# Dense stage of a graph-network kernel: one root computation for three groups, a chain spread over nine rounds, sums in six banks; counting and second edge layer rearranged

## The reference, cut to what matters

```python
h = jnp.maximum(_layernorm(x, axis=-1), 0.0)
x = x + _L0_gnn_ref(h, edge_index, edge_attr_32, ...)   # messages, gates, update, LayerNorm with gain and shift
h = jnp.maximum(_layernorm(x, axis=-1), 0.0)
x = x + _L1_gnn_ref(h, ..., edge_attr_96, src, dst)     # relu(e @ Wm1 + bm1) @ Wm2 + bm2, times the drop mask, summed by dst
h = jnp.maximum(_layernorm(x, axis=-1), 0.0)
x = x + _L2_gnn_ref(h, edge_index, L2_gnn_W, L2_gnn_b)  # mean over in-edges
h = jnp.maximum(_layernorm(x, axis=-1), 0.0)
x = x + _L3_gnn_ref(h, src, dst, ...)                   # three convolutions with degree norms
```

## Time and profile before

| | us |
|---|---|
| median of 3 runs (lowest, highest) | 6119.12 (6116.01, 6123.38) |
| the profiled execution, its own time | 6117.6 |
| its span, first to last instruction | 6115.7 |
| PE, DVE, ACT, POOL busy in the span | 4559.9, 4229.4, 3505.4, 3410.0 |

### The profile page before, as it was taken

The page is one execution under the profiler, slowest core; times in us unless marked ns, Lnnn a source line. Parts: engine busy times, 40 slices in busy tenths (PEclk is TensorE's granted clock), DMA queues, the critical chain, the costliest instruction groups (busy, mean ns, idle before and its releaser), DMA issues. The chain is left out here.

```text
span 6115.7 us, 115642 instructions
## 1 busy us (share of the span) xinstructions
PE 4559.9 (75%) x22351; PEld 2931.6 (48%) x22351; DVE 4229.4 (69%) x13899; ACT 3505.4 (57%) x8824; POOL 3410.0 (56%) x3543
## 2 busy tenths in 40 slices
PE   5776888888799999799999788878888984222222
PEld 1223555555444444466666566656656663222221
DVE  5667888888788888777777688878876663222222
ACT  6996666666699999555555455545545552111110
POOL 0004666666654443344343566566657776777777
PEclk9999999999999999899999787778778885555555
DMA  0002333333344443455555577656657773222222
GB/s 18 0 0 67 101 105 102 104 103 105 98 96 94 94 94 86 105 143 142 141 142 137 150 188 193 181 148 163 163 144 183 184 187 89 61 64 66 63 67 57
DMA packets 1144861, 677.32 MB, mean 111 GB/s; under 512 B 898421, under 2 KB 1096833, under 8 KB 1144744
## 3 DMA queue, kind: packets, MB, share of 16 engines
q1 hardware_dynamic: 1031784, 527.07, 31.7%
q0 software_dynamic: 112960, 148.99, 11.7%
HBM read 445.59 MB, written 232.61 MB: 111 GB/s over the span
## 5 line engine op out<-in xcount | busy, mean ns | idle before, releaser
L724 POOL DMA_INDIRECT xs<-t,idx x1176 | 1110.5, 944 | 951.5 <-DMA idx<-at 573.4
L1197 PE MATMUL bank<-ident,msg 128*96 128x128 f32 (+1 forms) x1568 | 305.5, 329 | 856.5 <-ACT msg L992 771.8
L724 POOL DMA_INDIRECT xs<-c,idx x784 | 763.9, 974 | 291.6 <-issue 233.2
L992 ACT ACTIVATE msg<-xs,now 128x96 f32<-128x96 f32 x784 | 229.3, 364 | 1071.4 <-DMA xs<-c,idx 715.3
L1041 PE MATMUL bank<-cols,before 128*128 128x384 f32 x1756 | 734.0, 520 | 17.3 <-DVE wu_out L1334 14.1
L1495 DVE TENSOR_TENSOR_SCAN aggT<-goes,aggT,bank 96x512 f32<-96x512 f16 (+1 forms) x490 | 620.7, 1267 | 133.9 <-PE bank L1150 115.0
L1197 PEld LDWEIGHTS bank<-ident,msg 128*96 128x96 f32 (+1 forms) x1568 | 218.6, 163 | 1022.7 <-ACT msg L992 650.1
L1208 PE MATMUL bank<-w,aggT 96*128 96x96 f32 (+1 forms) x3136 | 549.9, 334 | 105.2 <-DVE aggT L1495 104.6
L1670 DVE SCALAR_TENSOR_TENSOR y<-bank,now,rows 128x96 f32<-128x96 f32 x392 | 97.2, 310 | 719.1 <-PE bank L1208 719.1
L724 POOL DMA_INDIRECT xd<-in_x_dram,idx x392 | 373.9, 954 | 395.5 <-DVE xn L1565 228.6
L1208 PEld LDWEIGHTS bank<-w,aggT 96*128 96x128 f32 (+1 forms) x3136 | 517.3, 249 | 130.9 <-issue 88.6
(11 more groups left out here) (233 smaller groups left out, 10943.2 us busy)
## 6 DMA issues: line engine op xcount, KB each, us to landing
t<-xn SPq DMA_DIRECT2D x294, 192.0 KB, 2.2
xd<-t SPq DMA_DIRECT2D x294, 192.0 KB, 3.5
goes<-goes_d SPq DMA_DIRECT2D x392, 128.0 KB
xd<-in_x_dram SPq DMA_DIRECT2D x196, 192.0 KB
t<-xo SPq DMA_DIRECT2D x196, 192.0 KB
hd<-t SPq DMA_DIRECT2D x196, 192.0 KB
hs<-t SPq DMA_DIRECT2D x196, 192.0 KB
c<-xn SPq DMA_DIRECT2D x196, 192.0 KB
```

The source lines that it names most:

```text
L724: nc.gpsimd.indirect_dma_start(out=into, out_offset=None, in_=table, in_offset=bass.IndirectOffsetOnAxis(ap=indices, axis=0)).then_inc(don ...
L1197: ins = nc.tensor.transpose(bank[g.at(2)][0:m, c * P:(c + 1) * P], msg[:, g.at(2), c, 0:m], ident[:])
```

## The change

Counting: the high part of the destination is made by DVE in one `is_equal` of 128 columns, as the third instruction of `one_hot`. ACT keeps one Square and one Relu of 128 columns for the source.

Dense: the moments go to `dense_mv`, and `dense_roots` runs once for three groups, over the x of three groups and the y of three groups (24 columns). The lags grow: PE's and ACT's chain by three rounds, `mom_y` to 5, `norm_y` to 8, the last additions to 9, the store to 13. The relative order within the round on ACT and on PE is as it was. The sums stand in six banks (2 to 7); the two fillers write banks 0 and 1, each after a wait of its own. `plus_x` adds x from a second load, `dense_res_load`, into `hs` (three slots); the first load buffer is free after `norm1`.

Second edge layer: `messages` makes the product with features on partitions (one 96x512 product); PE's `turn_drop` transposes the drop mask into bank 5 instead of the messages, ACT's `drop_copy` copies it to SBUF, between hidden and home; `times_drop` multiplies there, and `sums` reads its result from SBUF.

```diff
             def dense_load(g):
-                need(sp, dn["xr"], g.j - 5)
+                need(sp, dn["norm"], g.j - 5)
...
+            def dense_res_load(g):
+                need(sp, dn["xr"], g.j - 2)
+                sp.sem_inc(sp_turn, 1)
+                sp.dma_start(hs[:, g.at(3), :, 0:D], node_view(a["x"], node_start(g.j))).then_inc(dn["res"][g.at(3)].sem, 16)
...
-            pipelined(sp, NG, [(info_idx, 0), (dense_load, 1), (x_src_store, 5), (info_keep, 6), (dense_store_x1, 8)])
+            pipelined(sp, NG, [(info_idx, 0), (dense_load, 1), (x_src_store, 5), (info_keep, 6), (dense_res_load, 9), (dense_store_x1, 13)])
...
                     if ph is e0:
                         need(sp, ph["tr_s"], g.j - 2)
                     else:
-                        need(sp, ph["msg"], g.j - 2)
+                        need(sp, ph["seg"], g.j - 2)
...
+            need(sp, dn["xr"], NG)
             edge_phase(e0, t1, 1, 11)
...
-                for which in range(2):
-                    ins = nc.scalar.activation(apart[:, g.at(2), which, :], iota_hi[:], ACT.Square,
-                                               bias=hi_of[:, which, bass.ds(g.j, 1)], scale=-1.0)
-                ins.then_inc(hot_his, 1)
+                nc.scalar.activation(apart[:, g.at(2), 0, :], iota_hi[:], ACT.Square,
+                                     bias=hi_of[:, 0, bass.ds(g.j, 1)], scale=-1.0).then_inc(hot_his, 1)
                 need(act, hot_his, 2 * g.j + 1)
-                nc.scalar.activation(hot_hi[:, g.at(2), :, :], apart[:, g.at(2), :, :], ACT.Relu, bias=1.0, scale=-1.0)\
+                nc.scalar.activation(hot_hi[:, g.at(2), 0, :], apart[:, g.at(2), 0, :], ACT.Relu, bias=1.0, scale=-1.0)\
                     .then_inc(hot_his, 1)
...
-            pipelined(act, NG, [(gelu1, 1), (norm1, 0), (norm_y, 2), (evac1, 0)])
+            pipelined(act, NG, [(gelu1, 4), (norm1, 3), (norm_y, 8), (evac1, 3)])
...
+                def drop_copy(g):
+                    need(act, ph["seg"], g.j + 1)
+                    need(act, ph["msg"], g.j - 1)
+                    nc.scalar.activation(tanh_g[:, g.at(2), :], bank[5][0:D, :], ACT.Copy).then_inc(ph["gate"].sem, 1)
...
-                    pipelined(act, EG, [(update_act, 4), (hidden, 2), (home_act, 1), (norms, 0), (evac_s, 0)])
+                    pipelined(act, EG, [(update_act, 4), (hidden, 2), (drop_copy, 2), (home_act, 1), (norms, 0), (evac_s, 0)])
...
             def dense_busy(g):
-                keep_busy(BUSY)
+                need(pe, dn["r1"], g.j)
+                nc.tensor.matmul(bank[0][:, 0:BUSY], before[:], steady[:, 0:BUSY], start=True, stop=True)
+
+            def dense_busy_too(g):
+                need(pe, dn["g1"], g.j)
+                nc.tensor.matmul(bank[1][:, 0:BUSY], before[:], steady[:, 0:BUSY], start=True, stop=True)
...
-            pipelined(pe, NG, [(out1, 1), (dense_busy, 0), (tr1, 0), (dense_busy, 0), (z1, 0)])
+            pipelined(pe, NG, [(out1, 4), (dense_busy, 3), (tr1, 3), (dense_busy_too, 3), (z1, 3)])
...
                     need(pe, ph["act"], g.j + 1)
+                    products(bank[2][0:D, :], wm2[:], m1[:, g.at(2), :], ph["tok"])
+
+                def turn_drop(g):
+                    need(pe, ph["attr"][g.at(3)], attr_landed(g))
+                    need(pe, ph["gate"], g.j)
                     for c in range(G):
-                        ins = nc.tensor.matmul(tok(bank[2])[:, c, :], m1[:, g.at(2), c * P:(c + 1) * P], wm2[:],
-                                               start=True, stop=True)
-                    ins.then_inc(ph["tok"].sem, 1)
-
-                def turn_messages(g):
-                    need(pe, ph["msg"], g.j + 1)
-                    need(pe, ph["agg"], g.j)
-                    for c in range(G):
-                        ins = nc.tensor.transpose(bank[5][0:D, c * P:(c + 1) * P], msg[:, g.at(2), c, 0:D], ident[:])
+                        ins = nc.tensor.transpose(bank[5][0:D, c * P:(c + 1) * P], drop[:, g.at(3), c, :], ident[:])
                     ins.then_inc(ph["seg"].sem, 1)
...
-                    pipelined(pe, EG, [(upd_z, 4), (hid, 2), (turn_messages, 3), (home_z, 1), (upd_u, 4), (messages, 2),
-                                       (home_u, 1), (tr, 0)])
+                    pipelined(pe, EG, [(upd_z, 4), (hid, 2), (home_z, 1), (upd_u, 4), (messages, 2),
+                                       (home_u, 1), (turn_drop, 1), (tr, 0)])
...
+                nc.vector.tensor_scalar(hot_hi[:, g.at(2), 1, :], iota_hi[:], hi_of[:, 1, bass.ds(g.j, 1)], None,
+                                        ALU.is_equal).then_inc(hot, 1)
...
+            def dense_roots(g):
+                if g.c % GT == GT - 1:
+                    b = half(g)
+                    roots(dense_mv[:, b, :, :, :].rearrange("p q c f -> p (q c) f"),
+                          steps_of(6 * G) + (dense_rstd[:, b, :, :].rearrange("p q c -> p (q c)"),
+                                             dense_nmr[:, b, :, :].rearrange("p q c -> p (q c)")),
+                          upto(g, NG, (dn["norm"], g.j - 5), (dn["norm_y"], g.j - 10), (dn["mx"], g.j + 1), (dn["my"], g.j - 4)),
+                          dn["root"], ROOT * g.use(GT))
...
-                nc.vector.tensor_tensor(xn[:, g.at(6), :, :], yx[:], xd[:, g.at(6), :, :], ALU.add)\
+                nc.vector.tensor_tensor(xn[:, g.at(6), :, :], yx[:], hs[:, g.at(3), :, 0:D], ALU.add)\
...
-            pipelined(dve, NG, [(times_g(dn), 4), (plus_x, 4), (plus_b, 4), (mom_x, 0), (mom_y, 2),
-                                (roots_of(dn, dense_state, kinds=2), 0, NG + 2)])
+            pipelined(dve, NG, [(times_g(dn), 9), (plus_x, 9), (plus_b, 9), (mom_x, 0), (mom_y, 5), (dense_roots, 0, NG + 5)])
...
                 def times_drop(g):
                     need(dve, ph["tok"], g.j + 1)
-                    need(dve, ph["attr"][g.at(3)], attr_landed(g))
+                    need(dve, ph["gate"], g.j + 1)
                     dve.sem_inc(dve_turn, 1)
-                    need(dve, ph["seg"], g.j - 1)
-                    nc.vector.tensor_tensor(msg[:, g.at(2), :, 0:D], tok(bank[2]),
-                                            drop[:, g.at(3), :, :], ALU.mult).then_inc(ph["msg"].sem, 1)
+                    need(dve, ph["agg"], g.j - 1)
+                    nc.vector.tensor_tensor(msgT[:, g.at(2), :], bank[2][0:D, :], tanh_g[:, g.at(2), :], ALU.mult)\
+                        .then_inc(ph["msg"].sem, 1)
...
-                    sums = sums_of(ph, lambda g: bank[5][0:D, :], ph["seg"], D, ph["z"])
+                    sums = sums_of(ph, lambda g: msgT[:, g.at(2), :], ph["msg"], D, ph["z"])
```

More of the change, by code:

```diff
@@ L240, in build @@
         mv = sb("mv", [P, 3, 3, G, 3])
[L241 to L245, removed]
+        var = sb("var", [P, 6 * G])
+        guess = sb("guess", [P, 6 * G])
+        sq = sb("sq", [P, 2, 6 * G])
+        res = sb("res", [P, 2, 6 * G])
+        root1 = sb("root1", [P, 6 * G])
         rstd = sb("rstd", [P, 3, 3, G])
@@ L844, in norm1 @@
             def norm1(g):
-                need(act, dn["root"], ROOT * (g.j + 1))
+                b, first = half(g), g.c % GT * G
+                need(act, dn["root"], ROOT * (g.use(GT) + 1))
                 need(act, dn["t1"], g.j - 2)
-                normed(hd[:, g.at(3), :, :], xd[:, g.at(6), :, :], g.at(3), 0).then_inc(dn["norm"].sem, 1)
+                for c in range(G):
+                    ins = nc.scalar.activation(hd[:, g.at(3), c, :], xd[:, g.at(6), c, :], ACT.Relu,
+                                               bias=dense_nmr[:, b, 0, first + c:first + c + 1],
+                                               scale=dense_rstd[:, b, 0, first + c:first + c + 1])
+                ins.then_inc(dn["norm"].sem, 1)
             def node_norm(g):
@@ L869, in norm_y @@
             def norm_y(g):
-                standard(dn, g, tok(bank[2 + 4 * g.at(2)]), 2, 1)
+                made = g.shift(5)
+                b, first = half(made), made.c % GT * G
+                need(act, dn["root"], ROOT * (made.use(GT) + 1))
+                need(act, dn["yx"], g.j - 1)
+                for c in range(G):
+                    ins = nc.scalar.activation(yg[:, g.at(2), c, :], tok(bank[2 + g.at(6)])[:, c, :], ACT.Identity,
+                                               bias=dense_nmr[:, b, 1, first + c:first + c + 1],
+                                               scale=dense_rstd[:, b, 1, first + c:first + c + 1])
+                ins.then_inc(dn["norm_y"].sem, 1)
             def evac1(g):
@@ L1017, in count @@
             def count(g):
-                need(pe, hot, 2 * (g.j + 1))
+                need(pe, hot, 3 * (g.j + 1))
                 need(pe, hot_his, 2 * (g.j + 1))
@@ L1059, in out1 @@
                 need(pe, dn["g1"], g.j + 1)
-                need(pe, dn["norm_y"], g.j - 1)
+                need(pe, dn["norm_y"], g.j - 5)
                 for c in range(G):
```

(14 more changed lines are left out.)

14 lines of the change are left out of this document (9 added, 5 removed).

## The result

| | us |
|---|---|
| before, median (lowest, highest) | 6119.12 (6116.01, 6123.38) |
| after, median of 5 runs (lowest, highest) | 6084.17 (6082.09, 6090.73) |
| ratio, with its 95% interval | 0.9946 (0.9931 to 0.9960) |
| span of the profiled execution, before and after | 6115.7, 6082.3 |

A forecast was written before the change was run, and what follows sets the result against it. Bounds: ACT in counting, rings of PE and ACT in dense and second edge layer. Terms -24 + 5 - 20 = -39 us from 6117.6 give 6079, and 6080 as median; 8-in-10 range 6035 to 6130.

The forecast's parts named there:

- the ring of PE and ACT: Dense: `gelu1`, `out1`, filler, `tr1`, `evac1`, `z1` closes on PE and ACT without DVE, 5.69 us, mean 5.76 a round.
- the path over home: Second edge layer: home starts 0.21 us earlier, norms follow, PE's wait falls from 0.55 to 0.34, 20 us less.
- DVE's own round with its gap: Counting: DVE done at 0.90 plus a gap of 0.16 makes 1.06 us a round instead of 1.12, 24 us less.
- the two-buffer ring: Counting: DVE and PE handing two buffers back and forth take 2.10 us for two rounds, 1.05 each.
- Rival 2: Counting: DVE becomes the bound if its third instruction with gap exceeds 0.36 us; at 0.42 total 6159; 11 in 100.
- The part about the ends: Dense: first roots need three groups' moments and three groups follow the last roots, together 5 us more.
- is what it was, only three rounds later: Dense: the order on ACT and PE is unchanged; the fillers keep their length and their new waits are already passed.
- a round or more early: Dense: second load, SP's extra issue and `dense_load`'s new wait for `norm1` all come a round or more early.
- a possible gain of 14 us: Dense: the ring could lose its slips, 5.76 to 5.69 us a round, 14 us less.
- DVE's relief costed at nothing: Dense: batched roots take 1.25 us a group off DVE, some 245 us, worth no time since DVE isn't in the ring.
- rival 1: Dense follows DVE after all and falls until POOL bounds it at 5.05 us a group: 139 us less, some 5940; 9 in 100.
- Rival 3: Counting and second edge layer: other links hold the old pace, nothing moves within 12 us, 6119; 14 in 100.

The follow-up runs named there:

- the kernel with swapped waits: The changed kernel with the two waits of `out1` and of `gelu1` in the other order, early one first: 6088.74 us, 0.9954 of before.
- the one with single waits: The changed kernel with `out1` waiting for `gelu1` alone and `gelu1` for `z1` alone, early waits moved elsewhere: 6062.99 us, 0.9909 of before.
- the ring was cut: The changed kernel with PE doing `tr1` of the next group before `out1`, and ACT `evac1` right behind `gelu1`: 5943.73 us, 0.9721 of before.

## Why the prediction was right, and where it was not

**Which chain bounds each stage** was right in dense, the ring of PE and ACT, and in the second edge layer, the path over home. In counting the forecast took DVE's own round with its gap, 1.06, and had the two-buffer ring that came 0.01 behind it. Each was shown by an experiment or by the wait that ends last, and none is one engine at work without a pause.

**The total was in part luck.** 6084 is 4 us from 6080, but the stages lie at -22, +18 and -25 where -24, +5 and -20 were forecast, and together 11 us short of the forecast. In the profiled executions 7 us of scatter behind them make up for most of that.

**Counting, -24 forecast, -21.6 measured.** The one unknown, the third instruction, was taken at 0.22 us from the nearest 128-wide row and measured 0.25. DVE's two rounds carry it to a round of 1.065 us instead of 1.06, by the ring of two buffers, not by the gap of 0.16: that gap isn't there any more (300.29 + 0.25 to 300.59 is 0.05). The Trainium skill's figures (VectorE: DVE Perf Modes, section on the TRN2 errata), 0.09 us and the estimate of 0.19, are both below the trace's 0.25. Rival 2 needed 0.36 and did not come.

**Dense, +5 forecast, +18.3 measured.** This is the mis-sized term. The part about the ends was near, 6.7 us for 5: the last `gelu1` to the end of the last addition takes 13.53 us instead of 9.22, 4.3 more, and the start up to the first `gelu1` 2.4 more. The step that failed is the sentence that the order on ACT and PE "is what it was, only three rounds later", so that the ring keeps its length. The order of the work is the same, but the waits are not issued the same way: in the changed kernel the value of `out1`'s wait for `norm_y` is computed ahead of `out1` in all six rounds of a turn instead of two, and the late wait for `g1` moves onto the register instruction. No run shows which part of the dense change makes it so. That is 0.08 us in four rounds of six of the loop. Of the 11.65 us by which the 195 rounds grew, this is about 8.4; the other 3.2 are the first round.

That first round took 8.90 us instead of 5.69, with PE's granted clock at 0.50 (the lower of its two levels, 1.2 GHz) from 499 to 513 us, where in before it had a mean of 0.78 in the ten microseconds around the first `gelu1`; in both PE had been busy 1.62 of the 15 us ahead of that. It doesn't go with the dense change: the kernel with swapped waits and the one with single waits had a first round of 5.69, and the dense stage of before had one of 9.04 in the kernel without the dense change. But four traces of the changed dense stage whose first round took 5.69 have a third round of 6.4 to 7.1 instead, at the full clock. In the kernel with single waits (7.10) ACT's `norm1` waits 2.37 us there for the second roots, and DVE before them for the load of group 5, which SP, in its order, issues only at 513.65, after waits of up to 6.8 us for what POOL fetches. Before, group 3 didn't have to wait for group 5's x. So the sentence that the new loads and waits are "a round or more early" fails at the start of the stage; in the profiled run the slow first round hides it.

The forecast had seen the slips of 5.76 to 5.85 in before and put them down as a possible gain of 14 us; they were the trace of the very mechanism that then grew.

**DVE's relief costed at nothing** was right, and rival 1 fell: 43 us less of DVE's work in 200 changes no round. (The root instructions have 24 columns, not the 12 of the row that the forecast took them from; they take 0.18 us instead of 0.17.) But the size of rival 1 was right as well. Once the ring was cut, the stage fell to 5.12 us a group, POOL's 5.05 and a little, and to 5944 us, where that rival said 5940. Its condition was wrong, not its price.

**Second edge layer, -20 forecast, -24.65 measured.** The mechanism came as described: the copy fits into ACT's idle time, home moves up, PE's wait falls, the mask's transfer isn't waited for. The copy holds ACT for 0.47 us from start to start instead of the 0.50 reckoned, home moves up 0.24 instead of 0.21, and the round gains 0.25. Rival 3 fell with it.

Left open: why the first dense round finds the lower clock in some executions and not in others. Of the eleven kernels with the uncut ring five have it (8.70 to 9.04 us), one execution each: the changed one and four others. The two with both counting and dense as before are not among them.

## What to carry to other kernels

Ask what ring a stage runs in before relieving its busiest engine: DVE was above 80% busy, and 29% less of its work was worth nothing until the order on PE and ACT was changed, one line on each; then it was worth 33 us. In a ring in which every link waits, look at how the late wait is issued: let it stand alone on its instruction, and put the waits that have long passed on an instruction with time to spare, at a place where computing their values hides. And when a copy is added to a chain, look for the place in the round where its input is already there but nobody waits behind it.

## What the runs showed of the hardware that was not expected

Where the semaphore that comes last is awaited not by the instruction that it releases but by one ahead of it, that costs 0.06 to 0.09 us each time. `out1` starts 0.05 us after `gelu1`'s end where its own weight load carries the late wait, 0.13 where a register instruction does, 0.14 to 0.15 where a separate wait does. On ACT a register instruction costs 0.08 and a separate wait 0.06. It was the same at three places, without an exception in the dense rounds of the four traces compared (before, changed, swapped waits, single waits). An `is_equal` of DVE against a column pointer takes 0.25 us at 128 columns of 16 bits and 0.42 at 784. And PE's granted clock can stay at 0.50 through the first dense round, which then takes 8.7 to 9.0 us instead of 5.69 with nearly the same instructions. Later in the stage it fell to 0.50 in single rounds, which took 7.4 to 7.5 us (mean clock of the round 0.77): in three of before, three of the changed kernel, nine of the one with swapped waits, none of the one with single waits. At some 1.7 us each they may be a good part of the scatter between executions; that isn't shown, since one execution of each kernel was profiled.
